# Two products per head moved from POOL to VectorE in a decoder layer's self-attention

## The reference

```python
q, k, v = (proj(Wq), proj(Wk), proj(Wv))          # 16 heads of 64
scores = jnp.einsum('bhqd,bhkd->bhqk', q, k)
scores = scores + bias.transpose(2, 0, 1)[None]    # by bucket of the distance
attn = jax.nn.softmax(scores, axis=-1)
ctx = jnp.einsum('bhqk,bhkd->bhqd', attn, v)
```

## Time and profile before

| | |
|---|---|
| median of 3 runs | 3798.07 us (3797.63 to 3800.9) |
| profiled execution | 3797.64 us |
| its span, first to last instruction | 3795.8 us |
| PE busy | 3681.4 us, 97% |
| POOL busy | 2684.2 us, 71% |
| DVE busy | 2450.3 us, 65% |
| ACT busy | 2016.1 us, 53% |
| mean granted TensorE clock | 0.989 of full speed |
| POOL L354 (acc) | 894 instructions, 2385 ns each |
| DVE L947 (maxima) | 1024 instructions, 1223 ns each |
| POOL L329 (the product) | 63 instructions, 1282 ns in the median, 1267 to 1294 |

### The profile page before, as it was taken

The page is one execution under the profiler, slowest core; times in us unless marked ns, Lnnn a source line. Parts: engine busy times, 40 slices in busy tenths (PEclk is TensorE's granted clock), DMA queues, the critical chain, the costliest instruction groups (busy, mean ns, idle before and its releaser), DMA issues. The chain is left out here.

```text
span 3795.8 us, 62609 instructions
## 1 busy us (share of the span) xinstructions
PE 3681.4 (97%) x21277; PEld 2195.6 (58%) x21277; DVE 2450.3 (65%) x3356; ACT 2016.1 (53%) x3452; POOL 2684.2 (71%) x1402
## 2 busy tenths in 40 slices
PE   9989999999999999999999999999979999997899
PEld 7755545555555555554555555555438888884387
DVE  3456676666666766776667776677526777774731
ACT  3336566666666665666666665666534555553232
POOL 1119999999999999999999999999963434430010
PEclk9989999999999999999999999999989999998999
DMA  7662223432234352243223333233322333335710
GB/s 222 160 145 64 70 70 82 103 76 69 70 74 106 100 139 70 70 106 83 72 68 71 99 89 72 67 72 89 92 79 76 104 97 106 105 125 197 248 37 23
DMA packets 368346, 366.60 MB, mean 97 GB/s; under 512 B 189339, under 2 KB 261531, under 8 KB 362776
## 3 DMA queue, kind: packets, MB, share of 16 engines
q1 hardware_dynamic: 299064, 336.50, 32.9%
q10 hardware_dynamic: 67168, 20.98, 2.4%
q0 software_dynamic: 1920, 6.29, 0.5%
HBM read 142.64 MB, written 89.70 MB: 61 GB/s over the span
## 5 line engine op out<-in xcount | busy, mean ns | idle before, releaser
L354 POOL TENSOR_TENSOR acc<-acc,probs 128x1024 f32<-128x1024 f32 x894 | 2131.8, 2385 | 147.0 <-ACT probs L822 35.5
L947 DVE TENSOR_REDUCE maxes<-ps 128x2 f32<-128x1024 f32 x1024 | 1251.3, 1223 | 474.2 <-PE ps L617 462.2
L825 ACT ACTIVATE probs<-ps,far_bias 128x1024 f32<-128x1024 f32 (+7 forms) x1280 | 999.0, 819 | 722.2 <-DVE near_s L964 447.1
L648 PE MATMUL ps<-probs,v_head 128*64 128x512 f32 x4096 | 993.7, 606 | 0.4 <-ACT probs L822 0.4
L636 PE MATMUL ps<-stacks 64*128 64x512 f32 x6144 | 810.9, 392 | 6.1 <-ACT probs L822 5.3
L636 PEld LDWEIGHTS ps<-stacks 64*128 64x128 f32 x6144 | 579.9, 186 | 133.3 <-ACT probs L822 12.6
L617 PE MATMUL ps<-stacks 64*128 64x512 f32 x2048 | 504.1, 490 | 17.5 <-DVE maxes L947 12.2
L617 PEld LDWEIGHTS ps<-stacks 64*128 64x128 f32 x2048 | 191.5, 184 | 565.1 <-DVE maxes L947 424.2
L648 PEld LDWEIGHTS ps<-probs,v_head 128*64 128x64 f32 x4096 | 248.6, 136 | 443.2 <-issue 441.8
L964 DVE TENSOR_TENSOR near_s<-ps,near_bias 128x384 f32<-128x384 f32 (+2 forms) x576 | 265.0, 491 | 37.2 <-PE ps L636 34.3
L970 DVE TENSOR_TENSOR c_q<-ps,c_q 64x512 fp32r<-64x512 f32 x128 | 87.5, 684 | 306.6 <-ACT c_q L781 306.6
(11 more groups left out here) (278 smaller groups left out, 4557.6 us busy)
## 6 DMA issues: line engine op xcount, KB each, us to landing
stacks<-c_q SPq DMA_DIRECT2D x128, 256.0 KB, 4.3
stacks<-c_d SPq DMA_DIRECT2D x64, 512.0 KB, 6.9
stacks<-c_k SPq DMA_DIRECT2D x32, 768.0 KB, 5.6
stacks<-c_k SPq DMA_DIRECT2D x64, 384.0 KB, 7.2
scr_v<-probs ACTq DMA_DIRECT2D x32, 512.0 KB, 4.1
v_head<-scr_v SPq DMA_DIRECT2D x32, 512.0 KB, 3.7
scr_ctx<-ctx_out SPq DMA_DIRECT2D x128, 128.0 KB, 2.3
both_ctx<-scr_ctx SPq DMA_DIRECT2D x32, 512.0 KB, 3.9
```

The lines of the kernel that those rows point to most:

```text
L354: pool.tensor_tensor(acc[:, qb, :], acc[:, qb, :], pr, ALU.add).then_inc(s["summed"], 1)
L648: mm = pe.matmul(ps[64 * half:64 * half + 64, PV, :], v_head[:, side, kt, :], probs[:, st % PT_RING, half * 512:(half + 1) * 512], start=k ...
L825: ins = act.activation(probs[:, st % PT_RING, a:z], sc[:, a:z], ACT.Exp, bias=bias)
L947: dve.tensor_reduce(maxes[:, qt:qt + HALF_GROUPS // 2 + 1:HALF_GROUPS // 2, first_chunk + pair], ps[:, bank:bank + 2, :], AX.X, ALU.max).t ...
```

## The change

The call of `context` leaves POOL's loop over the steps and enters DVE's loop over the groups. It stands behind the second reduction of the group (and `step` and `step_lo`, which don't fall in these groups) and ahead of `queries_low`. For qb = 0 it moves from step 25 to group 14 (steps 28 and 29) of head n, for qb = 1 from step 13 to group 6 (steps 12 and 13) of head n + 1. Waits, operands and the semaphore that it raises stay the same.

```diff
-CONTEXT_STEPS = {25: 0, 13: 1}
+CONTEXT_GROUPS = {14: 0, 6: 1}
...
 # POOL
-            def context(n, qb):
-
-                pool.wait_ge(s["recip_in"], 64 * n + 32 * qb + 32)
-                pool.wait_ge(s["ctx_raw"], 2 * n + qb + 1)
-                pool.tensor_tensor(ctx_out[:], ctx_out[:], sums[:], ALU.mult).then_inc(s["ctx"], 1)
...
-                    if st in CONTEXT_STEPS:
-                        of = CONTEXT_STEPS[st]
-                        if of == 0 or carry:
-                            context(n if of == 0 else n - 1, of)
...
 # DVE
+            def context(n, qb):
+
+                dve.wait_ge(s["recip_in"], 64 * n + 32 * qb + 32)
+                dve.wait_ge(s["ctx_raw"], 2 * n + qb + 1)
+                dve.tensor_tensor(ctx_out[:], ctx_out[:], sums[:], ALU.mult).then_inc(s["ctx"], 1)
...
                     if lowered:
                         step_lo(*lowered)
+                    if g in CONTEXT_GROUPS:
+                        qb = CONTEXT_GROUPS[g]
+                        if own if qb == 0 else carry:
+                            context(n if qb == 0 else n - 1, qb)
                     if prep and g in EVAC_GROUPS:
                         queries_low(n + 2, EVAC_GROUPS[g])
```

## The result

The changed kernel takes 3806.93 us in the median of 15 runs (3799.85 to 3810.47), the kernel before 3798.68 in 15 runs beside it (3794.74 to 3802.29): ratio 1.0021, 95% interval 1.0013 to 1.0029. That is 8.3 us slower, inside the range of the forecast (3794 to 3813) and 4 us above its value. The profiled execution took 3808.48 us, 10.8 more than that of before.

The account below looks back on a forecast made before the run. PE was taken to bound the middle heads, POOL's chain the end. Tail -1.7, head 13 +5.0 and +1.4, head 14 +0.7, others 0 gave +5.4 us on 3797.64: 3803 us, range 3794 to 3813.

Parts of the forecast that it names:

- What bounds the kernel: Middle heads: PE busy for all 79.50 us, so freeing POOL gives nothing; POOL's chain sets only the end.
- The product as an instruction that waits for POOL: On DVE: 0.69 us by itself, up to 3.1 us when issued during a POOL acc, whose end it must await.
- Rival 1: DVE and POOL don't hold each other up: +0.5 us in all, 3798.1 us; chance 0.2.
- Rival 3: DVE isn't let in between two accs and waits one more: 3922 us, or 3875 for group 6 alone; chance 0.07.
- The hard edge and its cover: Groups 6 and 14, middle heads: DVE's lateness for the next maximum costs PE equally; the product just fits, late by 0.
- Rival 4: Group 6's edge is missed by 0.1 to 0.4 us in each head: 3806 to 3815 us; chance 0.1.
- Head 13: Group 6: DVE waits for reciprocal copies queued behind the xn reload; the maximum and PE are 5.0 us late.
- the term for the slow matmuls behind it: Head 13, after PE's wait: matmuls run slower until the old pace is back, adding 1.4 us.
- The tail: Heads 30 and 31: removing POOL's products gains 3.7 us, less pushes and a late step 24: net 1.7 us gained.
- the push of POOL by a product: End, after step 24: each of three DVE products delays POOL's next acc by 0.55 us, 1.65 together.
- Head 14: Group 6: blocking by POOL makes the maximum 0 to 1.85 us late, mean 0.7 us.
- Its store, some 7 us later on SP than now, is still ahead of the next fill: 0: Group 14, middle head: the later context store still precedes the fill, which waits for the head's last scores; cost 0.

Follow-up runs that it names:

- e7: The changed kernel with the product replaced by a maximum with one SBUF input, behind the same waits: 3803.68 us, ratio 1.0012 to the kernel before.
- e10: The changed kernel with two SP requests moved in head 13 and the product behind queries_low: 3858.34 us, ratio 1.0159 to the kernel before.
- e8: The changed kernel with the product on DVE only in heads 30 and 31, on POOL elsewhere: 3795.68 us, ratio 0.9990 to the kernel before.
- e5: The changed kernel; in head 13 SP requests xn's first block behind the reciprocals' copies, its last ahead of the store: 3793.69 us, ratio 0.9986.
- e6: The kernel before; in head 13 SP requests xn's first block behind the reciprocals' copies, its last ahead of the store: 3796.61 us, ratio 0.9995.
- e2: The changed kernel with only group 14's product on DVE, that of step 13 back on POOL: 3798.58 us, ratio 0.9999 to the kernel before.
- e11: The kernel before, with head 13's last xn block requested only after the scores of step 30, store unmoved: 3804.61 us, ratio 1.0008.
- e12: The kernel before, with head 13's context store held on SP until the last projection is done: 3803.04 us, ratio 1.0002.

## Why the prediction held, and the step that failed

- **What bounds the kernel**: right. The length is unchanged in 27 heads, to 0.24 us; POOL's relief is worth nothing there.
- **The product as an instruction that waits for POOL**: right, in length and place: 2.73 and 2.07 us in the sampled head where the steps gave 2.7 and 2.1, never over 3.1; e7 shows that it is the second SBUF input. Rival 1 falls. Rival 3 falls too: DVE was let in at the end of the acc that ran when it asked, 62 times of 62. The Trainium skill's rule (SBUF — State Buffer, "Who interferes with whom") that issue order decides who blocks held.
- **The hard edge and its cover**: right. Group 6 kept 0.15 us to spare in the sampled head, and 1.0 in most; e10 shows the price once it is missed. Rival 4 falls.
- **Head 13**: mechanism and place right. The wait of PE was 5.0 by the steps and 4.82 in the trace. Mis-sized is the term for the slow matmuls behind it: 1.4 against 7.5 - 4.8 = 2.7. It was taken from an idle of 2.51 us after which matmuls were slow for some 3.1 us; here the clock stayed at half for some 5.7 us, which at half speed costs about the 2.7.
- **The tail**: mechanism right, size too small: -1.7 by the steps, -2.9 in the profile and -2.9 to -3.2 in timed medians (e8 against the kernel before, e5 against e6). The term that was mis-sized is the push of POOL by a product, three times 0.55; it measures about 0.25, and with that the same sum gives -2.6. POOL's busy time shows it as well: 60.7 us less (2684.2 to 2623.5) where 81 was forecast, and the longer accs are some 16 of the difference. That the profile's own figure comes out near is in part chance: PE waited 1.1 us less for the fill in head 30 than in that of before, and its last sums ran at the half clock. PE lost 1.98 us in head 30, group 6, where 1.5 was worked out.
- **Head 14**: the step that failed. The 0.7 us for blocking in group 6 was 0 (e5), and the 6.4 us contradict the step "Its store, some 7 us later on SP than now, is still ahead of the next fill: 0". The store is ahead of the fill, but in head 13 the last block of the reload stands between them, and it is what was pushed. The prediction weighed the store against the instruction two places behind it, in a middle head where the place between is empty. With 6.4 in the place of 0.7 the sum would have been about 3808 to 3809, the profile's own time. The sign that the idle of head 13 would be the only long one before 2660 failed with it. The profiled execution was 10.8 us slower where 5.4 was forecast; that the timed medians are only 8.3 apart, closer to the forecast, may owe something to runs without the whole of the late fill, as in e2; nobody foresaw that, and as far as the forecast goes it is luck.
- **Chances**: the change was given 0.28 to be slower by more than 0.2%, and 0.69 to be the same. The measured ratio, 1.0021, is just beyond the mark, and its interval lies on both sides of it.

## What to carry to other kernels

A wait that moves to an in-order engine is priced by its latest arrival over all iterations, not by the typical one: here one head of 32, with a reload ahead of a small copy, cost more than the change could give. When an instruction is later, look at everything queued behind its store on the DMA-issuing engine in that same exceptional iteration; moving two requests gave the loss back. And an elementwise DVE instruction with two SBUF inputs beside a POOL that is busy back to back takes the rest of POOL's instruction on top: it belongs where DVE has that much idle time ahead of a hard edge.

## What the runs showed of the hardware

- A DVE product with two SBUF inputs and a POOL acc hold each other up at instruction grain in both directions, and 0.14 us between two POOL instructions is enough for DVE to get in: the product took 0.69 to 2.91 us, never two accs, and the acc behind it about 0.25 us more than its 2.38.
- How long the granted clock stays at half after an idle of PE didn't follow the idle's length: some 5.7 us from PE's restart after idles of 4.82 and 3.26 us (changed kernel, e7), some 4.2 us after 5.44 us (head 14 of the changed kernel), some 3.3 us after 2.51 us (head 30 before). Idles of up to 1.5 us (the 59 of e10) left it at full speed.
- With a 2 MB reload requested 3.7 us ahead of the 4 MB of fills, the last fill of c_k landed 19.0 to 19.9 us after the first fill's issue (seven profiles); with 3.3 us or less, 22.8 to 24.2 us (six profiles). The timed runs of three of the six (e2, e11, e12) lose less than their profiles.
